# Reciprocals by logarithm and exponential, a second bank for row maxima, and a regrouped expert stage, in a four-stage kernel on one core

## The reference

```
_L0_attn_ref   16 heads of 64, causal:  softmax(masked / 8) @ v, then W_O
_L0_ffn_ref     8 heads, experts in the projections (3 of 5 kept by gates), softmax attention
_L1_attn_ref   16 heads of 64, all keys: softmax(q k * 0.25 + bias[bucket(k - q)]) @ v, then Wo
_L1_ffn_ref    16 experts; each takes the 32 tokens of a sequence with the largest softmax over tokens,
               h = relu(tok w1 + b1); h = relu(h w2 + b2); out = (h w3 + b3) * vals; scatter-add to the tokens
```

## Time and profile before

| | |
|---|---|
| timed runs | 4802.87 us median (4802.52 to 4806.01), 3 runs |
| profiled execution | 4799.74 us; span of its trace 4798.0 us |
| busy share of the span | PE 87%, DVE 72%, POOL 58%, ACT 41% |
| s0, units in steady state | about 95 to 1285 us |
| s1 | about 1325 to 2810 us |
| s2, units in steady state | about 2890 to 4570 us |
| expert stage | 4615 to 4798 us |

### The profile page before, as it was taken

How to read it: one execution, slowest core, us unless ns; L and a number is a source line. 1 busy time by engine, 2 the same in 40 slices (tenths; PEclk the granted TensorE clock), 3 DMA queues, 4 the chain that set the end, 5 groups by cost and what they waited for, 6 DMA issues and landing times. The chain is left out here.

```text
span 4798.0 us, 63558 instructions
## 1 busy us (share of the span) xinstructions
PE 4155.6 (87%) x22714; PEld 2198.2 (46%) x22714; DVE 3469.9 (72%) x5821; ACT 1959.7 (41%) x3371; POOL 2801.1 (58%) x2036
## 2 busy tenths in 40 slices
PE   5999999999778898888899848999999999999947
PEld 3544454444355554454554424444444444444416
DVE  3777877877577766766776537887888788788735
ACT  2444443434355454454444313443444344444411
POOL 1655555556536775775776815665666566566710
PEclk6999999999979999999999859999999999999976
DMA  2000000000011000010000021211221112111020
GB/s 50 13 13 13 22 13 22 22 1 5 5 65 34 17 31 20 26 34 17 22 33 1 5 57 25 39 27 27 37 39 27 27 38 38 27 32 31 14 62 18
DMA packets 98042, 125.91 MB, mean 26 GB/s; under 512 B 28896, under 2 KB 76448, under 8 KB 97728
## 3 DMA queue, kind: packets, MB, share of 16 engines
q1 hardware_dynamic: 97728, 121.86, 11.7%
HBM read 103.69 MB, written 18.12 MB: 25 GB/s over the span
## 5 line engine op out<-in xcount | busy, mean ns | idle before, releaser
L777 POOL TENSOR_TENSOR s_psum_p<-s_psum_p,s_prob 128x1024 f32<-128x1024 f32 (+3 forms) x640 | 1350.5, 2110 | 415.5 <-ACT s_prob L524 376.7
L524 ACT ACTIVATE s_prob<-s_sT 128x1024 f32<-128x1024 f32 (+2 forms) x896 | 836.7, 934 | 970.5 <-DVE s_sT L658 478.5
L432 PE MATMUL s_pv<-s_prob,s_vp 128*64 128x512 f32 (+3 forms) x3584 | 888.9, 575 | 3.9 <-POOL s_prob L762 3.0
L777 POOL TENSOR_TENSOR s_psum_p<-s_prob 128x1024 f32<-128x1024 f32 (+1 forms) x128 | 286.9, 2241 | 573.7 <-ACT s_prob L524 571.0
L1657 POOL TENSOR_TENSOR s_psum_p<-s_psum_p,s_prob 128x1024 f32<-128x1024 f32 x192 | 464.2, 2417 | 197.1 <-ACT s_prob L1386 195.9
L663 DVE RECIPROCAL s_recip<-s_recip 128x128 f32<-128x128 f32 x512 | 481.1, 942 | 99.1 <-ACT s_recip L474 99.1
L388 PE MATMUL s_mx<-s_bh,s_ah 64*128 64x512 f32 (+3 forms) x1792 | 390.2, 430 | 183.4 <-DVE s_bm L599 84.5
L609 DVE CUSTOM_DVE_ANT_0 s_mx<-s_mx,s_strip 128x512 f32<-128x512 f32 x640 | 429.4, 712 | 111.8 <-PE s_mx L388 110.8
L1386 ACT ACTIVATE s_prob<-s_sT 128x1024 f32<-128x1024 f32 x256 | 262.7, 1026 | 451.9 <-PE s_sT L1243 451.8
L407 PE MATMUL s_sT<-s_ah,s_bh 64*128 64x512 f32 (+3 forms) x1792 | 414.4, 459 | 19.2 <-ACT s_prob L524 18.9
L599 DVE TENSOR_REDUCE s_bm<-s_mx 128x8 f32<-128x1024 f32 (+3 forms) x384 | 362.4, 944 | 48.9 <-PE s_mx L388 40.0
(11 more groups left out here) (235 smaller groups left out, 7963.7 us busy)
## 6 DMA issues: line engine op xcount, KB each, us to landing
s_strip<-bias_rows SPq DMA_DIRECT2D x256, 144.0 KB, 5.7
s_wr<-gated_weights SPq DMA_DIRECT2D x32, 960.0 KB, 4.8
s_near<-bias_rows SPq DMA_DIRECT2D x256, 48.0 KB, 2.0
x<-s_x SPq DMA_DIRECT2D x12, 512.0 KB, 3.2
s_x<-x SPq DMA_DIRECT2D x8, 512.0 KB, 5.2
gated_weights<-s_side_hi SPq DMA_DIRECT2D x8, 480.0 KB, 2.5
gated_weights<-s_side_lo SPq DMA_DIRECT2D x8, 480.0 KB, 2.9
s_x<-in_L_attn_x_dram SPq DMA_DIRECT2D x4, 512.0 KB, 4.4
```

Of the source, the lines that this page charges most:

```text
L432: last = mm(pv[heads(hd), lo:CH], vp[:, g % 2, j, heads(hd)], prob[:, k % PR, hd, lo:CH], start=j == 0, stop=end)
L524: nc.scalar.activation(prob[:, k % PR, :, lo:CH], sT[:, k % 2, :, lo:CH], ACT.Exp, scale=st.scale).then_inc(exp_done, 1)
L777: nc.gpsimd.tensor_tensor(out[:, :, lo:CH], src, p[:, :, lo:CH], ALU.add)\
```

## The change

In both pair stages: ACT copies a row sum to `recip` as before, and also takes its logarithm straight from `misc` into a new tile `guess` and then the exponential of minus that, which approximates the reciprocal r. DVE forms x*r and then (x*r - 2)*r, minus the reciprocal, over all 512 columns; normalize multiplies by -1 as well. There are two DVE instructions in place of four, in two units, and normalize comes in the third (before: the fifth). `misc` is free after the logarithm, not after the copy. In a unit with two chunks of maxima both come ahead of `values`; the first goes to the other scores tile, `sT[:, (k + 1) % 2]`, once exponential k - 1 is done, and the next unit's scores wait until DVE has read it.

In s2 alone: the `dcol` columns are copied by ACT in unit 8, the chunks of maxima end in unit 11 (before: 12), and the transpose is in unit 13 (before: 14). The chunks begin in unit 0 as before.

In `expert_stage`: experts go four at a time, with one layer of the next four ahead of the next layer of these; scaling and splitting follow for each four; all `place` matrices are made during this; the scatter has the results as weights and 512 columns of `place` moving, so that its output is transposed and has to be copied by ACT and turned back by PE; the sum of squares of the layer norm is done on ACT in eight instructions with an accumulator, and the four sequences overlap.

```
-        self.mt_unit = 10 if causal else 14          # mx_steps: [1,1,1,1,1,1,2,1,2,1,2,1,1,0,0,0]
+        self.mt_unit = 10 if causal else 13          #           [1,1,1,1,1,1,2,2,2,2,1,1,0,0,0,0]
...
                     copy(recip[:, s % 2, :], misc[:, :]).then_inc(rs_read, 1)
+                    nc.scalar.activation(guess[:, s % 2, :], misc[:, :], ACT.Ln).then_inc(log_done, 1)
+                    act.wait_ge(log_done, s + 1)
+                    nc.scalar.activation(guess[:, s % 2, :], guess[:, s % 2, :], ACT.Exp, scale=-1.0)\
+                        .then_inc(guess_done, 1)
...
             def reciprocals(s, n):
-                dve.wait_ge(rs_read, s + 1)
-                cols = recip[:, s % 2, n * P:(n + 1) * P]
-                nc.vector.reciprocal(cols, cols).then_inc(recip_done, 1)
+                x, r = recip[:, s % 2, :], guess[:, s % 2, :]
+                if n == 0:
+                    dve.wait_ge(rs_read, s + 1)
+                    dve.wait_ge(guess_done, s + 1)
+                    tt(x, x, r, ALU.mult).then_inc(recip_done, 1)
+                else:
+                    dve.wait_ge(recip_done, 2 * s + 1)
+                    nc.vector.scalar_tensor_tensor(x, x, 2.0, r, ALU.subtract, ALU.mult).then_inc(recip_done, 1)
...
+                if other is None:
+                    pe.wait_ge(mx_read, banks)
+                    banks = NMX * g + n + 1
+                else:
+                    pe.wait_ge(exp_done, other)
+                    borrowed = NMX * g + n + 1
...
             def scores(g, u, k, c, j):
                 if k >= 2:
                     pe.wait_ge(exp_done, k - 1)
+                if borrowed is not None:
+                    pe.wait_ge(mx_read, borrowed)
...
+            def scatter(b):
+                if b >= 2:
+                    pe.wait_ge(yT_done, 2 * (b - 1))
                 pe.wait_ge(place_done, (b + 1) * EG)
+                for c in range(2):
+                    for eg in range(EG):
+                        cols = slice(c * CH, (c + 1) * CH)
+                        mm(big[:, b % 2, cols], rhi[:, eg, b, :], place[b][:, eg, cols], start=eg == 0, stop=False)
+                        last = mm(big[:, b % 2, cols], rlo[:, eg, b, :], place[b][:, eg, cols], start=False,
+                                  stop=eg == EG - 1)
+                    last.then_inc(y_full, 1)
```

More of the change, by code:

```diff
@@ L56 @@
 TOPS, TOPC = E0 + 1, 8 + 3 * (E0 - 1)
[L59 to L103, removed]
 class Pairs:
@@ L193, in jobs @@
             if s >= 0:
-                for n in range(4):
+                for n in range(2):
                     out[u + n].append(("recip", s, n))
-                out[u + 4 if u + 4 < self.U else u + 3].append(("norm", s))
+                out[u + 2].append(("norm", s))
         if p == 1 and b > 0:
@@ L304, in _ @@
             mm = nc.tensor.matmul
-            before = None
+            before = borrowed = None
+            banks = 0
             def misc_free():
@@ L457, in _ @@
                         misc_job(t)
-                for t in chunks[1:]:
-                    maxima(t[1], t[2])
                 if ("mt", g + 1) in todo:
@@ L2030, in _ @@
-                last.then_inc(y_full, 1)
+                    if i % 4 == 0:
+                        pe.wait_ge(yT_done, 2 * b + i // 4 + 1)
+                    last = nc.tensor.transpose(turned(b)[:, i * P:(i + 1) * P], xT[:, b % 2, i * P:(i + 1) * P],
+                                               cst.ident[:, :])
+                last.then_inc(t_full, 1)
+            first_layer(0)
+            for q in range(EG + 1):
+                if q + 1 < EG:
+                    first_layer(q + 1)
+                if q < EG:
+                    second_layer(q)
+                if q > 0:
+                    third_layer(q - 1)
@@ L2032, in _ @@
+            pe.wait_ge(rlo_done, EG)
+            for b in range(B + 1):
+                if b < B:
+                    scatter(b)
+                if b > 0:
+                    turn_back(b - 1)
         @block.scalar
@@ new lines, in second_layer, with high_part @@
+            def second_layer(q):
+                for e in range(4 * q, 4 * q + 4):
+                    act.wait_ge(l2, 4 * q + 4)
+                    if q >= 2:
+                        act.wait_ge(l3, q - 1)
+                    nc.scalar.activation(h2[:, e % 8, :], two[:, q % 2, e % 4 * P:(e % 4 + 1) * P], ACT.Relu,
+                                         bias=b2[:, e:e + 1]).then_inc(l2d, 1)
+            def high_part(q):
+                act.wait_ge(res_done, B * (q + 1))
+                nc.scalar.activation(rhi[:, q, :, :], res[:, q, :, :], ACT.Copy).then_inc(rhi_done, 1)
@@ new lines, in _, with squares @@
+            first_layer(0)
+            for q in range(EG + 2):
+                if q + 1 < EG:
+                    first_layer(q + 1)
+                if q < EG:
+                    second_layer(q)
+                if q >= 2:
+                    high_part(q - 2)
+            def squares(b):
+                act.wait_ge(sum_step, 3 * b + 3)
+                for i in range(NB):
+                    last = nc.scalar.activation(h1[:, i, :], xnew[:, b % 2, i, :], ACT.Square,
+                                                bias=sums[:, b % 2, 0, i:i + 1],
+                                                accum_out=sums[:, b % 2, 1, i:i + 1])
+                last.then_inc(square_done, 1)
@@ L2061, in _ @@
+            for b in range(B):
+                for c in range(2):
+                    cols = slice(c * CH, (c + 1) * CH)
+                    act.wait_ge(y_full, 2 * b + c + 1)
+                    if b >= 2:
+                        act.wait_ge(t_full, b - 1)
+                    nc.scalar.activation(xT[:, b % 2, cols], big[:, b % 2, cols], ACT.Copy).then_inc(yT_done, 1)
+                if b > 0:
+                    squares(b - 1)
+            squares(B - 1)
         @block.vector
```

254 lines of the change are left out of this document (151 added, 103 removed).

## The result

The changed kernel takes 5180.28 us (median of 4 runs, 5175.47 to 5184.15); the kernel before took 4804.44 us beside it (4802.52 to 4806.94). The ratio is 1.078, with an interval of 1.0763 to 1.0800. It is slower by 376 us. 4751 us and a range up to 4795 were forecast; the first rival (tables, 5000 us, chance 0.10) is what happened, and it cost more than that rival said.

What follows compares the result with a forecast made beforehand. PE was taken to bound s0 and s2, and the expert stage to run one thing after another. Expert stage -37, s0 -12, s2 0, stage ends -3 make -52 from 4799.7: 4748, plus 3.1 gives 4751 us, range 4700 to 4795.

Steps and rivals of the forecast that it cites:

- the first rival: Both pair stages: logarithm and exponential in different table sets, two loads a pass (2.57 us), 250 us, 5000 us; chance 0.10.
- (a): Expert stage, layers: four experts with a layer ahead take 21.7 us, saving 5.3; bounds are savings of 4 and 7.
- (b): Expert stage, between layers and scatter: 3.0 us stay of 12.25, saving 9 us, or 6 if DVE lags behind the layers.
- (c): Expert stage, scatter and layer norm: 41.6 us for 64.5, saving 23, with a DVE and ACT loop of 6.9 us a sequence.
- Second bank and moved jobs: Maxima chunks in s0 and s2: shorter PE waits less new ones, 12 us gained in s0, 0 in s2.
- Rival 3: Pair stages: most of PE's idle time before maxima goes, 115 us in place of 12, 4648 us; chance 0.13.
- The wait of 2.2 us: DVE in each pass: it waits about 2.2 us for the guess before its multiply, where it waited 0.93.
- Nothing stalls from that alone: Pair stages: unit 3's bias comes about 1 us late, but the scores needing its exponential come 2.3 us after it.
- rival 2: Pair stages: most new two-operand DVE instructions are held at the port by a POOL add, 4834 us; chance 0.12.

## Why the prediction was wrong

**The step that failed: the table loads.** The sum had logarithm and exponential at 0.6 us each, the guess ready 1.3 us after the copy, and nothing for table loads; rival 1 gave the loads a chance of 0.10 on the two pages named there. The Trainium skill, "ScalarE: Activation LUTs", Table sets, is right that one set has both: with it loaded, no pass had a load. But nothing chose that set: this program fetched a table for the logarithm and another for the exponential, 256 times in all, and the guess was ready after 3.85 us. Without the loads the kernel takes 471.6 us less. The trace of before had loads only about the sigmoid and none between copy and exponential; it was silent on what would be chosen for a logarithm, and 0.10 was too low.

**The rival was right in its cause and wrong in its path.** It charged ACT's queue, 2.57 less 0.5 us a pass, 250 us in all. ACT's 2.57 us are nearly free (9 us, moved behind the guess). What costs is that DVE, in its order, waits 4.5 us for the guess with the bias and the chunk behind it. The loads cost 3.7 us a pass (471.6 / 128), and 1.6 of them are longer matmuls (203 us of busy time, mostly by the lower clock), for which the rival had no term.

**Expert stage: 37 forecast, 47 found.** (a) Layers: 12.1 us (5113.16 to 5125.29) for the 21.7 of the sum; it kept 1.46 us for 16 matmuls of the third layer, but 32 now take 1.08, and the idle stretches between layers went as said. It saved 15, not 5, and lies outside the bounds of 4 and 7. (b) To the scatter: 6.8 us for 3.0; DVE did lag, with 18.2 us of work from the first layer to the scatter as forecast but only 12.1 us of layers to do it in; the bound of 6 was nearer (5.4 saved). (c) Scatter and layer norm: 38.0 us for 41.6. The 12 slow matmuls came as forecast, and so did the first sum, 10.8 us after the scatter's start (11); the loop is 6.0 and not 6.9 us a sequence (5142.94 to 5148.96), since eight squares with their accumulator reads go at 0.385 us each.

**Second bank and moved jobs: 12 us forecast for s0 and 0 for s2 together with the reciprocals; found without the loads 30 and 20, the difference of two wrong terms.** The bank, the steps and the column gave 65 us in s0 and 63 in s2 (128 alone), and the new reciprocals took back 36 and 44. The sum had put back, for new waits, most of what the second bank took away: 1.2 of 1.8 us a group in s0; in s2 0.85 and 1.15 at the scores, and 1.2 in units 3 to 5, for the 2.0 behind second chunks and the 0.42 at unit 15. In the kernel with the old reciprocals four short waits are left in an s2 group, 1.15 us of idle time for the 3.0 of before (50.85 less 47.92):

```profile
3030.78 0.50 PE L383 MATMUL s_sT<-s_ah,s_bh 64*128 64x512 f32 x2 [0.21 <-ACT s_prob L498]
3038.03 0.50 PE L358 MATMUL s_mx<-s_bh,s_ah 64*128 64x512 f32 x2 [0.42 <-DVE s_bm L603]
3052.58 0.50 PE L383 MATMUL s_sT<-s_ah,s_bh 64*128 64x512 f32 x2 [0.35 <-DVE s_bm L597]
3063.05 0.50 PE L383 MATMUL s_sT<-s_ah,s_bh 64*128 64x512 f32 x2 [0.17 <-DVE s_bm L603]
```

Rival 3 (115 us from the idle time before maxima, chance 0.13) was the right size for this part. Two of these four waits are scores that wait for a chunk's read, 0.52 us in all: the second chunk, values and a job have mostly covered it. The 2.2 us of the `dcol` copy, which the sum took off DVE, only passed to the instruction behind it.

**Reciprocals without loads.** The wait of 2.2 us came (2.1). That "Nothing stalls from that alone" was wrong: 80 us are lost beside the second bank, and with the three instructions a unit later they come back. The two new instructions were priced at 1.4 us each; they took 0.88 and 0.89 (0.69 and 0.94 with the loads), never under 0.67. So rival 2, the port, was not what cost here; with the instructions a unit later the Newton step is longer (1.29) and the kernel faster. What rival 2 described is still seen: normalize varies (0.68 to 2.90 us), and DVE's addition over 6 columns took 2.19 us at 3205.25. Each term on DVE was about a delay in an ordered queue; I priced its length and not what stood behind.

Without the loads the measured 4708.7 lies 42 us under the sum of 4751 and inside its range. That would have been partly luck: the second bank and the column gave 116 us more than the sum had for s0 and s2, the expert stage 10 more, and the reciprocals took 80 that the sum did not have.

## What to carry to other kernels

When an edit brings a new function to ScalarE, count the table loads in the built program before pricing it; if one set has all the functions of a loop, write out its load ahead of the loop (here 5180 us became 4709). An instruction that waits for another engine's result costs by what stands behind it in the same queue. Here 2.57 us a pass on ACT cost 9 us in all behind the value that DVE waits for, and 472 ahead of it. So issue the consumer a unit or two later than the earliest place, if nothing needs its result sooner. A second buffer for one of two chunks was worth 173 us in its place, more than any cheaper instruction around it. And taking a small instruction off an engine gains nothing if what held it holds the next one.

## What the runs showed of the hardware

- A table load (ACT_TABLE_LOAD) takes 1.28 us, and a switch of tables took no more than the load: from the end of the copy (3198.92) to the start of the logarithm (3200.23) 1.31 us pass, of which the load is 1.28.
- The clock's share of a stall can match the stall. Groups 568.80 and 1009.55 of the changed kernel have 215 matmuls and 5.4 us of idle time each; one runs at PEclk 1.00 and the other at 0.85, 5.9 us longer. Why it fell in the one and not in the other, these rows don't tell. With all 256 loads but no wait (DVE two units later) PE is busy 4091.8 us and not 4302.3.
- The third layer's 128x128 matmuls with 32 output rows: 16 took 1.53 us with four in a row on the same 32 rows, and 32 take 1.08 where each goes to the next 32 rows, a third of the time each (96 ns, 34 ns), at PEclk 1.00 both times. Order and count of experts changed together here, so it isn't shown that the order alone does it.
- An instruction of VectorE can take as long as GpSimd's add beside it. The addition of 6 columns took 154 ns behind a copy and 2.1 us where it came first, and it ended with POOL's add (3207.44 and 3207.41).
